# A selective-scan block on one core: step size and sums of states added by DMAs, x plus shift made in DRAM, a new timetable

## The chip, the core and the metric

The kernel runs on one core of one Trainium2 chip. The metric is the device time of one execution in microseconds (us); several executions are timed and their median is taken. The profile is of one further execution.

## What is computed

For four sequences of 4096 tokens with D = 512 channels, all in fp32:

```
h    = layernorm(x) * (1 + ca) + sa
xs,z = split(h @ w_in.T + b_in)
dt   = softplus(xs @ w_dt.T + b_dt);  Bm = xs @ w_B.T + b_B;  Cm = xs @ w_C.T + b_C
state[t] = exp(A*dt[t]) * state[t-1] + dt[t]*Bm[t]*xs[t]     (16 states per channel)
y    = sum over the 16 states of state[t]*Cm[t]  +  D*xs
x1   = x + ga * (layernorm((y*silu(z)) @ w_out.T + b_out + h) * gamma + beta)
out  = x1 + gb * (small feed-forward of layernorm(x1)*(1+cb)+sb)
```

## The kernel before, in words

The tokens are cut into 32 chunks of 512 (`NCH`), four blocks of 128 tokens each (`TB`), and the channels into four groups of 128 (`KD`). The scan of a chunk is U = 64 units, one for each of 16 states times four channel groups. For unit i:

- ACT makes the decay exp(A*dt) (`decays`, L915) five units ahead, and the input dt*xs*B in token-major form (`input_of`, L925);
- PE turns that input to channel-major form by four 128x128 transposes into PSUM (`turn_v`, L526 into `b_ps`). There are two buffers, so the transposes of unit i+1 wait for the scan of unit i-1;
- DVE scans (L1219), and keeps the last state of each pair (L1227);
- Pool multiplies two units at a time by C (`product`, L411) into the ring `pr` of 12 units.

The sum over the states goes two ways. For the states in `HELD`, the product of state n is not sent to PE: an accumulating DMA that Pool issues (`add_products`, L422, two units of 512 KB in all) adds it to the product of state n+1. What is left is added by PE as accumulating transposes into `y_ps` (`add_unit`, L601), four 128x128 instructions for each unit in `ADDS`: 40 units of a chunk. D*xs is added to state 3's product by DMAs too (`add_skip`, L429).

A step s scans chunk s, and beside it does the front of chunk f = s+1 (norm, `xs`, step size `dt`, B and C), the back of chunk b = s-1 (gate, `w_out`, second norm), and the feed-forward end of chunk c = s-2. All dense products run on PE in one fixed chain (`dense`). No scheduler orders this: every engine runs its 64 units in order, and a table of numbers says after which unit each other piece is put into the engine's program: `PE_AT` for PE's chain (`z.3.1@59` is the second product of z's fourth bank, after unit 59), `AT` for the rest. A piece stands in program order there, and everything behind it on its engine waits with it:

```
                for i in range(U):
                    if has_s and i + 1 < U:
                        turn_v(s, i + 1)
                    beside.until(i)
```

Three places the change touches:

- The step size. DVE makes max(v, 0) and -|v| (`take_dt`, L1290, L1296), ACT exp and ln of the second into `tmp` (`softplus`, L1057, L1060), Pool adds the halves (`step_size`, L474), then multiplies by xs (`inputs`, L485). PE turns the result (`turn_u`), DVE copies it (`take_u`, L1304), and ACT needs it for the first input of the next chunk.
- x plus shift. SP loads x again into `x1` (`loads`, L344), Pool issues two accumulating DMAs of the shift row (`shifted`, L446), waits for them and adds the attention part (`attended`, L454).
- The sums of states, above.

Of the kernel before, what the change touches and what calls it, by code (L numbers as in the profile page):

```python
def build_program(nc, ap, B, L, D, N, M, INNER):
# [46 lines left out]
    AT = dict(  # L48
        store=(0, 3, 5, 7),
        load=(2, 4, 8, 12),  # L50
        c_store=51,
        xsh=(13, 17),
        x1=(17, 17, 19, 19),
        bout=55,
        dt_add=(41, 42, 45, 49),
        u_mul=(43, 50, 50, 50),
        gate=(29, 60, 62, 6),
        relu=(61, 61, 0, 0, 0, 0, 0, 3),
        gm=4,
        skip=(6, 8, 9, 13),  # L60
        rstdx=11,
        xn=(11, 11, 11, 11),
        t2=(11, 13, 18, 21),
        rstd2=25,
        xn2=(25, 25, 25, 25),
        h2=(28, 32, 39, 42),
        h=(16, 20, 21, 22),
        xs=(25, 25, 26, 30),
        cb=50,
        bt=50,  # L70
        edt=(40, 43, 45, 50),
        ldt=(40, 43, 45, 50),
# [1340 lines left out]
```

## Time and profile before

| what | value |
|---|---|
| three timed executions | 4292.26, 4300.26, 4297.14 us; median 4297.14 |
| the profiled execution | 4280.81 us, its span 4279.1 us |
| granted TensorE clock, mean | 0.989 of full speed |
| busy share: PE, ACT, DVE, Pool | 96%, 89%, 85%, 83% |
| DMA traffic | 555.86 MB, mean 130 GB/s |

A busy share is a mean over the span, in which stretches with different limits lie. A row of a group of instructions gives line, engine, operation, tiles, count, busy time and the mean of one. A row of the timeline gives start and length; where the next row of the same engine starts sooner than the length says, instructions overlap, and the distance of the starts is what one costs.

### The profile page before, as it was taken

Reading aid. Unit: us, or ns where it says so; the run is one execution under the profiler, and the core shown is the slowest. Engines: PE = TensorE matmul, PEld = TensorE weight load, DVE = VectorE, ACT = ScalarE, POOL = GpSimd, SP = SyncE. Lnnn points to the kernel's source line nnn. Section 1 sums busy time; section 2 is a strip of 40 time slices with the busy share of each in tenths; the row PEclk is TensorE's granted clock in tenths of the full one; section 3 lists DMA queues with packets and bytes.
Section 4 is the critical chain, followed back from the end, with each engine's and each line's share of the span. In section 5 each row is a group of like instructions: output and inputs, shape, how many; then the busy total and the mean of one; then the engine's idle time right before and its main releaser. Section 6 shows DMA issues by size and latency. Waiting matters only on the chain. (4 is left out here: it accounts for less than half of the span.)

```text
span 4279.1 us, 70886 instructions
## 1 busy us (share of the span) xinstructions
PE 4100.2 (96%) x22688; PEld 2620.3 (61%) x22688; DVE 3643.8 (85%) x5134; ACT 3826.7 (89%) x6371; POOL 3558.1 (83%) x2090
## 2 busy tenths in 40 slices
PE   7999999999999999999999999999999999999987
PEld 3666666666666666666666666656666666666654
DVE  3788898888888888888888888888988888988884
ACT  3899999999999999998999999999999999999984
POOL 2888889888888888888888888988888888888883
PEclk8999999999999999999999999999999999999998
DMA  4456555656655666555666555665556675556663
GB/s 148 103 125 150 133 122 110 145 131 145 135 123 111 142 141 141 133 115 117 139 148 141 128 115 126 134 148 132 128 115 137 133 150 132 125 113 141 129 140 70
DMA packets 242537, 555.86 MB, mean 130 GB/s; under 512 B 29020, under 2 KB 31068, under 8 KB 242168
## 3 DMA queue, kind: packets, MB, share of 16 engines
q0 software_dynamic: 98816, 302.02, 39.1%
q1 hardware_dynamic: 143352, 249.29, 18.9%
q8 instruction: 185, 3.03, 0.3%
q14 instruction: 184, 1.51, 0.1%
HBM read 281.70 MB, written 34.64 MB: 74 GB/s over the span
## 5 line engine op out<-in xcount | busy, mean ns | idle before, releaser
L411 POOL TENSOR_TENSOR work<-work,c_bc 128x1024 f32<-128x1024 f32 x1024 | 2653.2, 2672 | 414.2 <-DVE work L1219 307.0
L1219 DVE TENSOR_TENSOR_SCAN work<-work,state,b_ps 128x512 f32<-128x512 f32 x1792 | 2245.6, 1272 | 242.2 <-PE b_ps L526 207.1
L925 ACT ACTIVATE work<-u_td,b_td 128x512 f32<-128x512 f32 x2048 | 1455.5, 711 | 114.7 <-PE b_ps L526 104.7
L915 ACT ACTIVATE work<-dt_t,neg_a 128x512 f32<-128x512 f32 x2048 | 1453.9, 710 | 17.1 <-DVE work L1219 14.7
L526 PEld LDWEIGHTS b_ps<-ident,work 128*128 128x128 f32 x8192 | 969.1, 141 | 645.1 <-issue 415.5
L526 PE MATMUL b_ps<-ident,work 128*128 128x128 f32 x8192 | 1229.1, 275 | 107.6 <-DVE work L1219 100.3
L601 PEld LDWEIGHTS y_ps<-ident,work 128*128 128x128 f32 x5120 | 585.9, 141 | 164.1 <-issue 157.1
L601 PE MATMUL y_ps<-ident,work 128*128 128x128 f32 x5120 | 673.4, 275 | 4.6 <-DMA work<-work 2.8
L675 PE MATMUL dense<-w_out_t,proj 128*128 128x512 f32 x1024 | 519.7, 606 | 0.0
L733 PE MATMUL dense<-xs_t,w_dt_t 128*128 128x512 f32 x1024 | 506.1, 593 | 0.0
L767 PE MATMUL dense<-h_t,w_in_t 128*128 128x512 f32 x1024 | 502.7, 593 | 0.0
L704 PE MATMUL dense<-h_t,w_in_t 128*128 128x512 f32 x1024 | 483.3, 595 | 1.0 <-ACT h_t L929 1.0
L422 POOL DMA_DIRECT2D work<-work x384 | 425.4, 1151 | 55.5 <-POOL work L411 46.5
L1219 DVE TENSOR_TENSOR_SCAN work<-work,b_ps 128x512 f32<-128x512 f32 x256 | 305.5, 1211 | 51.3 <-PE b_ps L526 49.8
L526 PEld LDWEIGHTS dense<-ident,xn 128*128 128x128 f32 x1536 | 187.7, 144 | 138.1 <-issue 88.1
L526 PE MATMUL dense<-ident,xn 128*128 128x128 f32 x1536 | 237.3, 279 | 34.1 <-ACT xn L1012 16.0
L474 POOL TENSOR_TENSOR dt_t<-dt_t,tmp 128x512 f32<-128x512 f32 x128 | 196.8, 1620 | 78.6 <-ACT tmp L1060 78.2
L704 PEld LDWEIGHTS dense<-h_t,w_in_t 128*128 128x128 f32 x1024 | 175.9, 191 | 127.7 <-issue 120.3
L947 ACT ACTIVATE tmp<-gm,b,w 128x512 f32<-128x512 f32 x256 | 196.4, 805 | 63.8 <-POOL sz_t L490 49.1
L675 PEld LDWEIGHTS dense<-w_out_t,proj 128*128 128x128 f32 x1024 | 162.1, 190 | 143.3 <-issue 143.3
L767 PEld LDWEIGHTS dense<-h_t,w_in_t 128*128 128x128 f32 x1024 | 167.1, 191 | 77.2 <-issue 67.7
L454 POOL TENSOR_TENSOR x<-x,tmp 128x512 f32<-128x512 f32 x128 | 206.9, 2006 | 2.3 <-DMA x<-par_d 2.3
(113 smaller groups left out, 4214.4 us busy)
## 6 DMA issues: line engine op xcount, KB each, us to landing
work<-work POOLq DMA_DIRECT2D x384, 512.0 KB, 5.7
c_bc<-c_d SPq DMA_DIRECT2D x512, 256.0 KB, 3.5
xn<-in_x SPq DMA_DIRECT2D x128, 256.0 KB, 5.1
work<-xs_t POOLq DMA_DIRECT2D x64, 512.0 KB, 5.9
x<-in_x SPq DMA_DIRECT2D x128, 256.0 KB, 4.4
x<-par_d POOLq DMA_DIRECT2D x64, 512.0 KB, 6.7
x<-par_d POOLq DMA_DIRECT2D x32, 1024.0 KB, 9.9
out_dram<-x SPq DMA_DIRECT2D x128, 256.0 KB, 4.2
```

Of the source, the lines that this page charges most:

```text
L411: gp.tensor_tensor(made_here, both(hs, HS_RING, s * U + i), c_bc[:, (s * N + n) % C_RING:(s * N + n) % C_RING + 1, :].to_broadcast([P, 2, ...
L422: gp.dma_start(both(pr, PR_RING, s * U + i), both(pr, PR_RING, s * U + i - KD), accum_op=ALU.add).then_inc(sum_done[i % KD // 2], Q)
L454: gp.tensor_tensor(x1[:, tb, :], x1[:, tb, :], tmp[:, tb, :], ALU.add).then_inc(S["x1_done"], 1)
L526: return nc.tensor.transpose(dst, src, ident[:, :])
L601: last = mm(y_ps[:, tb, j * P:(j + 1) * P], pr[:, (s * U + i) % PR_RING, tb * P:(tb + 1) * P], ident[:, :], is_transpose=True, start=(i == ...
L675: last = mm(long(s, "pre", tb)[:, :], yz_t[:, k, tb * P:(tb + 1) * P], w_out[:, k, :], start=False, stop=(k == KD - 1))
L704: last = mm(long(s, "xs", m)[:, :], w_in[:, k, m * P:(m + 1) * P], h_t[:, f % 2, k, :], start=(k == 0), stop=(k == KD - 1))
L733: last = mm(long(s, "dt", m)[:, :], w_dt[:, k, m * P:(m + 1) * P], xs_t[:, k, :], start=(k == 0), stop=(k == KD - 1))
L767: last = mm(long(s, "z", m)[:, :], w_in[:, k, D + m * P:D + (m + 1) * P], h_t[:, s % 2, k, :], start=(k == 0), stop=(k == KD - 1))
L915: A(decay[:, (s * U + i) % DEC_RING, :], dt_t[:, s % 2, j, :], ACT.Exp, scale=neg_a[:, j, n:n + 1]).then_inc(S["dec_done"], 1)
L925: A(v[:, n % V_RING, tb, :], u_td[:, tb, :], ACT.Copy, scale=b_td[:, s % 2, tb, n:n + 1]).then_inc(S["v_done"], 1)
L1219: V.tensor_tensor_scan(hs[:, (s * U + i) % HS_RING, :], decay[:, (s * U + i) % DEC_RING, :], b_ps[:, i % 2, :], state[:, i:i + 1] if s % N ...
```

## The change

1. `HELD` has eight states in place of six: 0, 1, 3, 4, 6, 7, 9, 10. So 16 accumulating DMAs of a chunk sum products in place of 12, and PE adds 32 units in place of 40.
2. The two halves of the step size are added by two accumulating DMAs of 512 KB each, issued by Pool, in place of four Pool instructions. Whoever waited for `dt_done` waits for `dt_added`.
3. x plus shift is made ahead in a DRAM buffer: at unit 40 of step s SP writes the shift row 512 times to DRAM (1 MB), at unit 59 Pool issues an accumulating DMA of x on it (1 MB, DRAM to DRAM), and in step s+1 SP loads the sum into `x1`. The two accumulating DMAs of `shifted` go.
4. All numbers of `PE_AT` and `AT` are new.

The diff, with most of the two tables left out:

```diff
--- before.py
+++ after.py
@@ -21,7 +21,7 @@
 
     V_RING, DEC_RING, HS_RING, PR_RING, C_RING = 2, 7, 6, 12, 3
 
-    HELD = (0, 1, 3, 4, 6, 8)
+    HELD = (0, 1, 3, 4, 6, 7, 9, 10)
     RELU_RING = 3
 
 
@@ -33,60 +33,61 @@
     GROUPS = ("g", "pre.0", "pre.1", "pre.2", "pre.3", "z.0", "xs.0", "xs.1", "xs.2", "xs.3", "dt.0", "dt.1", "dt.2",
               "dt.3", "cb", "z.1", "z.2", "s", "z.3")
     PE_AT = {}
-    for entry in """g.0@0 g.1@0 g.2@0 g.3@0 g.4@1 g.5@2 g.6@2 yz.0@2 g.7@3 res.0@3 yz.1@3 pre.0.0@4 yz.2@4 pre.0.1@5
...
-        z.1.1@49 bt.0@50 z.1.2@50 z.1.3@52 z.2.0@53 ut.0@55 z.2.1@55 z.2.2@55 ut.1@55 z.2.3@55 s.0@57 ut.2@57
-        s.1@57 s.2@57 ut.3@58 s.3@59 z.3.0@59 z.3.1@59 z.3.2@59 z.3.3@61""".split():
+    for entry in """g.0@0 g.1@1 g.2@3 g.3@3 g.4@8 g.5@8 g.6@8 yz.0@8 g.7@8 res.0@8 yz.1@8 pre.0.0@9 yz.2@9 pre.0.1@10
...
+        z.1.1@54 bt.0@55 z.1.2@56 z.1.3@57 z.2.0@58 ut.0@61 z.2.1@61 z.2.2@61 ut.1@61 z.2.3@61 s.0@62 ut.2@62
+        s.1@62 s.2@62 ut.3@62 s.3@62 z.3.0@63 z.3.1@63 z.3.2@63 z.3.3@63""".split():
         part, first = entry.split("@")
         PE_AT[part] = int(first)
     AT = dict(
-        store=(0, 3, 5, 7),
-        load=(2, 4, 8, 12),
-        c_store=51,
-        xsh=(13, 17),
-        x1=(17, 17, 19, 19),
...
-        dt_add=(41, 42, 45, 49),
-        u_mul=(43, 50, 50, 50),
...
-        xs=(25, 25, 26, 30),
...
-        y_copy=(1, 1, 1, 1),
-        yz=(2, 4, 5, 7),
...
-        dt=(35, 40, 43, 45),
-        ut=(54, 56, 57, 58),
...
-        stx=(0, 0, 6, 9),
...
+        store=(5, 10, 12, 17),
+        load=(11, 11, 15, 27),
+        c_store=45,
+        x1=(17, 19, 23, 28),
...
+        dt_add=(50, 53),
+        u_mul=(54, 56, 56, 56),
...
+        xs=(32, 35, 36, 39),
...
+        y_copy=(7, 7, 7, 7),
+        yz=(8, 9, 10, 11),
...
+        dt=(43, 47, 50, 53),
+        ut=(61, 61, 62, 62),
...
+        stx=(1, 8, 11, 11),
...
+        spread=40,
+        x_add=59,
     )
 
     def summed(n):
@@ -117,6 +118,7 @@
 
         par_d = nc.dram_tensor("par_d", (4, B, D), f32).ap()
         c_d = nc.dram_tensor("c_d", (2, N, T), f32).ap()
+        xsh_d = nc.dram_tensor("xsh_d", (2, TB, P, D), f32).ap()
 
         w_in = sb("w_in_t", [P, KD, 2 * D])
         w_dt = sb("w_dt_t", [P, KD, D])
...
@@ -341,8 +343,19 @@
                 for tb in range(TB):
                     yield AT["load"][tb]
                     sp.wait_ge(S[f"stored_{tb}"], at(f"stored_{tb}", c, Q))
-                    sp.dma_start(x1[:, tb, :], ap["x"][b * T + tb * P:b * T + (tb + 1) * P, :]
+                    sp.wait_ge(S["x_added"], (b + 1) * Q)
+                    sp.dma_start(x1[:, tb, :], xsh_d[b % 2, tb]
                                  ).then_inc(xb_loaded[tb], Q)
+
+            def spread_shift(s):
+                yield AT["spread"]
+                sp.wait_ge(S["par_stored"], 4 * Q)
+                if s >= 2:
+                    for tb in range(TB):
+                        sp.wait_ge(xb_loaded[tb], (s - 1) * Q)
+                sp.dma_start(xsh_d[s % 2].rearrange("b p d -> p b d"),
+                             par_d[1:2, s // NC:s // NC + 1, :].to_broadcast([P, TB, D])
+                             ).then_inc(S["shift_spread"], Q)
 
             def store_c(f):
                 yield AT["c_store"]
...
@@ -437,19 +452,17 @@
                     if summed(i // KD):
                         add_products(s, i)
 
-            def shifted(b):
-                for n in range(TB // 2):
-                    yield AT["xsh"][n]
-                    gp.wait_ge(S["par_stored"], 4 * Q)
-                    for tb in (2 * n, 2 * n + 1):
-                        gp.wait_ge(xb_loaded[tb], (b + 1) * Q)
-                    gp.dma_start(x1[:, 2 * n:2 * n + 2, :], par_d[1:2, b // NC:b // NC + 1, :].to_broadcast([P, 2, D]),
-                                 accum_op=ALU.add).then_inc(xsh_done[n], Q)
+            def add_x(s):
+                yield AT["x_add"]
+                gp.wait_ge(S["shift_spread"], (s + 1) * Q)
+                gp.dma_start(xsh_d[s % 2].rearrange("b p d -> p b d"),
+                             ap["x"][s * T:(s + 1) * T, :].rearrange("(b p) d -> p b d", p=P),
+                             accum_op=ALU.add).then_inc(S["x_added"], Q)
 
             def attended(b):
                 for tb in range(TB):
                     yield AT["x1"][tb]
-                    gp.wait_ge(xsh_done[tb // 2], (b + 1) * Q)
+                    gp.wait_ge(xb_loaded[tb], (b + 1) * Q)
                     gp.wait_ge(S["t2_done"], at("t2_done", b, tb + 1))
                     gp.tensor_tensor(x1[:, tb, :], x1[:, tb, :], tmp[:, tb, :], ALU.add
                                      ).then_inc(S["x1_done"], 1)
@@ -468,11 +481,11 @@
                 gp.tensor_tensor(wout_g[:, :], wout_g[:, :], wout_b[:, :], ALU.mult).then_inc(S["wout_done"], 1)
 
             def step_size(f):
-                for m in range(KD):
-                    yield AT["dt_add"][m]
-                    gp.wait_ge(S["ldt_done"], at("ldt_done", f, m + 1))
-                    gp.tensor_tensor(dt_t[:, f % 2, m, :], dt_t[:, f % 2, m, :], tmp[:, m, :], ALU.add
-                                     ).then_inc(S["dt_done"], 1)
+                for n in range(KD // 2):
+                    yield AT["dt_add"][n]
+                    gp.wait_ge(S["ldt_done"], at("ldt_done", f, 2 * n + 2))
+                    gp.dma_start(dt_t[:, f % 2, 2 * n:2 * n + 2, :], tmp[:, 2 * n:2 * n + 2, :], accum_op=ALU.add
+                                 ).then_inc(dt_added[n], Q)
 
             def inputs(f, b):
                 for m in range(KD):
...
@@ -910,7 +923,8 @@
                 n, j = i // KD, i % KD
                 if i == 0:
                     act.wait_ge(S["neg_done"], 2)
-                    act.wait_ge(S["dt_done"], at("dt_done", s, KD))
+                    act.wait_ge(dt_added[0], (s + 1) * Q)
+                    act.wait_ge(dt_added[1], (s + 1) * Q)
                 act.wait_ge(S["scan_done"], at("scan_done", s, i + 1 - DEC_RING))
                 A(decay[:, (s * U + i) % DEC_RING, :], dt_t[:, s % 2, j, :], ACT.Exp, scale=neg_a[:, j, n:n + 1]
                   ).then_inc(S["dec_done"], 1)
...
@@ -1314,7 +1328,7 @@
                     V.tensor_scalar(sz_t[:, m, :], bank[:, :], b_z[:, m:m + 1], None, ALU.add
                                     ).then_inc(S["zc_done"], 1)
                     if m:
-                        dve.wait_ge(S["dt_done"], at("dt_done", f, m + 1))
+                        dve.wait_ge(dt_added[m // 2], min(f + 1, NCH) * Q)
                     dve.wait_ge(S["x1_done"], at("x1_done", b, m + 1))
                     V.tensor_scalar(tmp[:, m, :], bank[:, :], b_z[:, m:m + 1], -87.0, ALU.add, ALU.max
                                     ).then_inc(S["zmax_done"], 1)
```

On PE, the end of one chunk and the first eight units of the next (`dense<-proj,win` is s, `dense<-h_t,w_in_t` z, `dense<-ident,xn` here the turn of u, `y_ps` the sum of states, `b_ps` the input of a unit, `dense<-tmp,w_dg` g). Before:

```order
L526 MATMUL dense<-ident,xn 128x128 x4
L526 MATMUL b_ps<-ident,work 128x128 x4
L791 MATMUL dense<-proj,win 128x512
L767 MATMUL dense<-h_t,w_in_t 128x512 x3
L526 MATMUL b_ps<-ident,work 128x128 x8
L767 MATMUL dense<-h_t,w_in_t 128x512
L601 MATMUL y_ps<-ident,work 128x128 x12
L526 MATMUL b_ps<-ident,work 128x128 x4
L601 MATMUL y_ps<-ident,work 128x128 x20
L526 MATMUL b_ps<-ident,work 128x128 x8
L623 MATMUL dense<-tmp,w_dg 64x256 x8
L601 MATMUL y_ps<-ident,work 128x128 x12
```

Eight units' sums (32 instructions) stand between z and g. In the change, the same place:

```order
L539 MATMUL b_ps<-ident,work 128x128 x4
L804 MATMUL dense<-proj,win 128x512
L539 MATMUL dense<-ident,xn 128x128 x4
L804 MATMUL dense<-proj,win 128x512 x2
L539 MATMUL dense<-ident,xn 128x128 x4
L804 MATMUL dense<-proj,win 128x512
L614 MATMUL y_ps<-ident,work 128x128 x4
L780 MATMUL dense<-h_t,w_in_t 128x512 x4
L614 MATMUL y_ps<-ident,work 128x128 x12
L539 MATMUL b_ps<-ident,work 128x128 x8
L636 MATMUL dense<-tmp,w_dg 64x256 x2
L539 MATMUL b_ps<-ident,work 128x128 x4
```

The products of s and z's last bank, and the turns of u, stand after units 61 to 63 now, with little between them but these; before, they were spread from unit 55 on. Behind them, in the change's first units of the next chunk:

```order
L636 MATMUL dense<-tmp,w_dg 64x256 x2
L539 MATMUL b_ps<-ident,work 128x128 x8
L636 MATMUL dense<-tmp,w_dg 64x256 x4
L539 MATMUL b_ps<-ident,work 128x128 x8
L614 MATMUL y_ps<-ident,work 128x128 x8
L539 MATMUL b_ps<-ident,work 128x128 x4
L614 MATMUL y_ps<-ident,work 128x128 x4
L539 MATMUL b_ps<-ident,work 128x128 x8
L636 MATMUL dense<-tmp,w_dg 64x256 x6
```

Half of g's products stand behind unit 8 now, and the turns of y behind them; before, all of g's products and the turns of y stood within the first eight units.

On Pool, the step size in the last third of a chunk. Before (`dt_t<-dt_t,tmp` is the add, `xn<-dt_t,xs_t` the product u, `work<-work,c_bc` the product of two units):

```order
L474 TENSOR_TENSOR dt_t<-dt_t,tmp 128x512 x2
L411 TENSOR_TENSOR work<-work,c_bc 128x1024
L485 TENSOR_TENSOR xn<-dt_t,xs_t 128x512
L411 TENSOR_TENSOR work<-work,c_bc 128x1024
L474 TENSOR_TENSOR dt_t<-dt_t,tmp 128x512
L411 TENSOR_TENSOR work<-work,c_bc 128x1024 x2
L474 TENSOR_TENSOR dt_t<-dt_t,tmp 128x512
L485 TENSOR_TENSOR xn<-dt_t,xs_t 128x512 x3
```

The products u follow their adds on the same engine, the last three directly. In the change, where the adds are DMAs:

```order
L487 DMA dt_t<-tmp 128x1024
L426 TENSOR_TENSOR work<-work,c_bc 128x1024 x2
L487 DMA dt_t<-tmp 128x1024
L498 TENSOR_TENSOR xn<-dt_t,xs_t 128x512
L426 TENSOR_TENSOR work<-work,c_bc 128x1024
L498 TENSOR_TENSOR xn<-dt_t,xs_t 128x512 x3
L426 TENSOR_TENSOR work<-work,c_bc 128x1024 x2
L474 DMA x<-par_d 128x4x512
L458 DMA xsh_d<-in_x 128x4x512
```

Three products u stand behind the second DMA, with one product of states between; the DMAs of the bias row and of x to DRAM follow together.

## Rows read from the trace of the kernel before

**Rows 1.** The page, engines: busy us, share of span, instructions.

```profile
PE 4100.2 (96%) x22688; PEld 2620.3 (61%) x22688; DVE 3643.8 (85%) x5134; ACT 3826.7 (89%) x6371; POOL 3558.1 (83%) x2090
```

**Rows 2.** One chunk in three stretches: stretch, length, busy by engine, clock, DMA share.

```profile
1629.41:1646.62 17.21, 14.81 (x105) 9.70 (x105) 17.02 (x25) 16.77 (x29) 11.31 (x7) 1.00 0.09 28
1646.62:1683.84 37.22, 37.22 (x163) 20.83 (x162) 33.38 (x52) 34.19 (x62) 29.10 (x22) 1.00 0.98 211
1683.84:1758.12 74.28, 74.16 (x444) 50.53 (x444) 63.28 (x85) 68.36 (x113) 70.91 (x42) 1.00 0.52 117
```

**Rows 3.** An instruction done once a chunk: first and last start.

```profile
L1046 ACT ACTIVATE cb_t<-dense,b_cb_col x32: 345/348/368, 57.9 to 4053.1; 128x128 f32<-128x128 f32 x32
```

**Rows 4.** Timeline of PE: start, length, what.

```profile
1499.88 2.22 PE L623 MATMUL dense<-tmp,w_dg 128*64 128x256 f32 x16
1502.03 1.53 PE L601 MATMUL y_ps<-ident,work 128*128 128x128 f32 x12
...
1604.13 0.60 PE L526 MATMUL b_ps<-ident,work 128*128 128x128 f32 x4
1604.57 1.02 PE L767 MATMUL dense<-h_t,w_in_t 128*128 128x512 f32 x2
1605.43 1.04 PE L601 MATMUL y_ps<-ident,work 128*128 128x128 f32 x8
```

**Rows 5.** Timeline of DVE, the same columns.

```profile
1637.88 2.44 DVE L1219 TENSOR_TENSOR_SCAN work<-work,state,b_ps 128x512 f32<-128x512 f32 x2
1640.24 0.13 DVE L1227 TENSOR_REDUCE state<-work 128x2 f32<-128x2 f32 x1
1640.29 0.68 DVE L1258 TENSOR_TENSOR proj<-sz_t,dense 128x512 f32<-128x512 f32 x1
1640.88 1.27 DVE L1219 TENSOR_TENSOR_SCAN work<-work,state,b_ps 128x512 f32<-128x512 f32 x1
```

**Rows 6.** Waits over the whole span: total us, times, longest.

```profile
POOL x L446 <- DMA x<-in_x: 116.5, 58, 12.4
...
DVE norm L1237 <- POOL x L454: 41.0, 33, 3.5
```

**Rows 7.** The page, DMA queues (share of 16 engines' span) and issues (us to landing).

```profile
q0 software_dynamic: 98816, 302.02, 39.1%
...
work<-work POOLq DMA_DIRECT2D x384, 512.0 KB, 5.7
...
x<-par_d POOLq DMA_DIRECT2D x32, 1024.0 KB, 9.9
```

**Rows 8.** Groups by line on Pool and ACT: busy us, mean ns, idle before.

```profile
L422 POOL DMA_DIRECT2D work<-work x384 | 425.4, 1151 | 55.5 <-POOL work L411 46.5 <-DMA work<-work 4.8 <-PE y_ps L601 3.3
L474 POOL TENSOR_TENSOR dt_t<-dt_t,tmp 128x512 f32<-128x512 f32 x128 | 196.8, 1620 | 78.6 <-ACT tmp L1060 78.2
...
L1057 ACT ACTIVATE tmp<-tmp,b_dt_col 128x512 f32<-128x512 f32 x128 | 91.3, 713 | 8.3 <-DVE tmp L1296 8.3
...
L1060 ACT ACTIVATE tmp<-tmp 128x512 f32<-128x512 f32 x128 | 80.9, 632 | 4.1
```

**Rows 9.** Timeline of Pool at the start and in the tail.

```profile
60.30 1.26 POOL L474 TENSOR_TENSOR dt_t<-dt_t,tmp 128x512 f32<-128x512 f32 x1 [2.45 <-ACT tmp L1060]
...
4246.71 2.48 POOL L454 TENSOR_TENSOR x<-x,tmp 128x512 f32<-128x512 f32 x2 [2.33 <-DMA x<-par_d]
```

**Rows 10.** Stretches of the second chunk's start, columns as in rows 2.

```profile
213.40:219.50 6.10, 2.85 (x21) 2.17 (x21) 6.03 (x12) 2.60 (x5) 2.36 (x1) 0.98 0.31 86
219.50:222.80 3.30, 3.30 (x17) 3.30 (x18) 3.30 (x5) 3.27 (x6) 1.54 (x1) 0.53 0.00 0
222.80:240.00 17.20, 15.33 (x75) 9.03 (x74) 16.58 (x27) 15.55 (x28) 14.55 (x10) 1.00 0.64 149
```

**Rows 11.** Timeline of PE in that low stretch.

```profile
219.49 1.09 PE L526 MATMUL b_ps<-ident,work 128*128 128x128 f32 x4 [0.62 <-DVE work L1219]
...
221.22 1.06 PE L526 MATMUL dense<-ident,dt_t 128*128 128x128 f32 x4
```

More of the change, by code:

```diff
@@ L67, in build_program @@
-        h=(16, 20, 21, 22),
-        xs=(25, 25, 26, 30),
[L69 to L72, printed above, removed]
-        ez=(24, 57, 57, 4),
-        lz=(24, 57, 57, 4),
-        sig=(24, 57, 57, 5),
-        y_copy=(1, 1, 1, 1),
-        yz=(2, 4, 5, 7),
-        out=(9, 10, 11, 13),
-        pre=(9, 11, 14, 18),
-        dt=(35, 40, 43, 45),
-        ut=(54, 56, 57, 58),
-        z=(21, 53, 56, 61),
-        s=59,
-        stx=(0, 0, 6, 9),
-        nmrx=10,
@@ L86, in build_program @@
-        st2=(23, 23, 23, 24),
-        nmr2=25,
-        y=(14, 14, 18, 24, 28, 28, 34, 34, 36, 37, 40, 40, 45, 46, 46, 46, 46, 46, 46, 47, 47, 51, 52, 52, 54, 54, 55, 56, 57, 61, 61, 61, 62, 62, 62, 62, 62, 64, 64, 64),
-        sum=(6, 8, 9, 11, 13, 17, 17, 20, 21, 25, 30, 32, 39, 40),
+        store=(5, 10, 12, 17),
+        load=(11, 11, 15, 27),
+        c_store=45,
+        x1=(17, 19, 23, 28),
+        bout=59,
+        dt_add=(50, 53),
+        u_mul=(54, 56, 56, 56),
+        gate=(42, 62, 63, 8),
@@ new lines, in build_program @@
+        relu=(62, 63, 1, 1, 3, 7, 7, 7),
+        gm=7,
+        skip=(0, 3, 8, 12),
+        rstdx=14,
+        xn=(14, 14, 15, 16),
+        t2=(17, 18, 23, 24),
+        rstd2=33,
+        xn2=(33, 33, 33, 33),
+        h2=(38, 40, 44, 49),
+        h=(23, 25, 26, 29),
+        xs=(32, 35, 36, 39),
+        cb=54,
+        bt=54,
+        edt=(49, 50, 50, 52),
+        ldt=(49, 50, 50, 52),
+        ez=(39, 58, 60, 8),
+        lz=(39, 58, 60, 8),
+        sig=(39, 58, 60, 8),
+        y_copy=(7, 7, 7, 7),
@@ new lines, in build_program @@
+        yz=(8, 9, 10, 11),
+        out=(12, 14, 16, 20),
+        pre=(12, 17, 21, 23),
+        dt=(43, 47, 50, 53),
+        ut=(61, 61, 62, 62),
+        z=(27, 58, 61, 63),
+        s=62,
+        stx=(1, 8, 11, 11),
+        nmrx=13,
+        st2=(21, 31, 31, 31),
+        nmr2=32,
+        y=(16, 16, 20, 21, 30, 31, 31, 33, 41, 42, 43, 44, 52, 52, 52, 53, 53, 54, 55, 58, 59, 59, 59, 60, 61, 62, 63, 63, 63, 69, 69, 70),
+        sum=(5, 7, 10, 12, 13, 18, 18, 21, 23, 26, 29, 31, 34, 37, 42, 43, 45, 47),
@@ L200, in build_program @@
         w2dg_done b_out_loaded bout_done moved_ps moved c_exp c_one c_rcp silu_c rows_ps rows_taken mods_ps mods_done sign_done gate_done par_made
-        par_stored bout_row bout_made bout_added gs_loaded wg_loaded wout_done sign_set""".split()
+        par_stored shift_spread x_added bout_row bout_made bout_added gs_loaded wg_loaded wout_done sign_set""".split()
         PER = {
             "SP": dict(stored_0=Q, stored_1=Q, stored_2=Q, stored_3=Q, c_stored=TB * Q),
-            "Pool": dict(prod_done=U // 2, x1_done=TB, dt_done=KD, u_done=KD, sz_done=KD),
+            "Pool": dict(prod_done=U // 2, x1_done=TB, u_done=KD, sz_done=KD),
             "PE": dict(b_made=U, y_added=len(ADDS), s_ps=1, g_used=J, yz_ps=KD, out_ps=TB, res_used=TB, pre_ps=TB, xt_ps=KD, xs_ps=KD,
@@ L361, in step @@
                     chains.append(loads(b, c))
+                if has_s:
+                    chains.append(spread_shift(s))
                 if has_f:
```

37 lines of the change are left out of this document (13 added, 24 removed).

## The prediction

> **What bounds the kernel now.** I read the engines' shares first: PE is busy 96% of the span, ACT 89%, DVE 85%, Pool 83% [rows 1]. That makes PE the suspect but says nothing of where. So the next view is the table of stretches, cut for one chunk at the starts of the scans of units 0, 8 and 24 and of the next chunk's unit 0 [rows 2]. It shows three limits. In units 0 to 7 (17.2 us) DVE is busy 17.0 and PE 14.8. In units 8 to 23 (37.2) PE is busy throughout and the DMA engines are at 0.98. In units 24 to 63 (74.3) PE is busy 74.2 and the DMA share is 0.52. A chunk takes 128.7 us there; over the run it is (4053.1 - 57.9) / 31 = 128.9 [rows 3].
>
> PE's and DVE's work can be counted out of the two tables of numbers. What one piece costs is the distance of starts in the timelines. On PE: four 128x128 turns or sums of a unit 0.43 to 0.44, a 128x512 product (two records) 0.86, one of g's eight parts 2.15 / 4 = 0.54 [rows 4]; an `out` product I put at 1.05, since it stands between changes of tile. On DVE: a scan with its share of the state copy (1640.29 - 1637.88) / 2 = 1.2, a multiply or copy of 128x512 0.59 [rows 5]; estimates beside these are 0.87 for a pair of moments, 0.67 for the scaling behind, 1.3 for the two reads of a bank of dt or z; the counts below bear them out. Before:
> - units 0 to 7: PE 16 groups of four, 2 products, 8 of g = 13.0; DVE 8 scans, 8 copies, 3 moments = 17.1. Measured 17.2.
> - units 8 to 23: PE 26 groups, 23 products, 4 `out` = 35.4; DVE 32.9. Measured 37.2, so 1.8 is lost.
> - units 24 to 63: PE 82 groups, 43 products, B and C = 74.4; DVE 61.6. Measured 74.3.
> So the larger of PE and DVE in each stretch, plus 1.8, gives the chunk. PE and DVE can't borrow from each other over more than two units, since the transposes of unit i+1 wait for the scan of unit i-1.
>
> **The change part by part.**
> *Two more states summed.* PE loses 8 units of 4 instructions: 8 x 0.437 = 3.5 us a chunk, the only work that leaves PE. Pool issues four more DMAs, at most 1.15 us each [rows 8]; traffic grows by 2 MB a chunk.
> *Step size by DMA.* Four Pool adds of 1.62 [rows 8] become two issues. Over the whole change Pool gets five issues more (four sums, two step sizes, x, less the two of the shift), 5.8 us, and loses 6.5: no difference on an engine with 111 of 128.7 busy [rows 2]. What counts is latency. A DMA of that size from Pool lands 5.7 us after its issue [rows 7], where an add took 1.26 [rows 9]. Behind the second one stand three products u, which PE's turn of u and so everything of units 61 to 63 waits for. PE has 21 groups, 5 products, and B and C between the last product of dt (unit 52) and that turn: 9.2 + 4.3 + 1.4 = 14.9 us. The chain beside it is DVE 1.3, exp and ln 0.71 + 0.63 [rows 8], issue 1.15 [rows 8], landing 5.7, and three products at the add's 1.26 = 13.3, plus up to 3.7 for a scan and a product of states that are in front. Slack is 1.6 to -2.1; I take it as hidden, with a stall of 0 to 2.
> *x plus shift ahead.* Two accumulating DMAs of 512 KB leave the crowded stretch; 1 MB to DRAM by SP at unit 40 and 1 MB of accumulation at unit 59 come where the share was 0.52 [rows 2]. No row shows a DRAM-to-DRAM accumulation. Bounds: nothing, and the 9.9 us of the 1 MB one into SBUF [rows 7] once more; it has some 25 us until the load that waits for it, so both ends are hidden and I take 0. Pool stops waiting for x (116.5 us in all) and DVE's moments for x1 (41.0, or 1.3 a chunk) [rows 6].
> *Traffic.* The software queue used 39.1% of 16 engines for 302 MB [rows 7], 5.5 us for each MB. Units 8 to 23 lose the shift's 1 MB, one sum and a load, so their share falls from 0.98 to near 0.8; units 24 to 63 gain four sums, two step sizes and x, 4 MB or 22 us, beside SP's 1 MB, and go from 0.52 to near 0.8.
> *The timetable.* The dense chain starts some seven units later and ends at unit 63. Counted as above, after:
> - units 0 to 7: PE 11 groups and 4 of g = 7.0; DVE 8 scans, 4 copies, 1 moment = 12.9.
> - units 8 to 23: PE 29 groups, 17 products, 4 of g, 4 `out` = 33.7; DVE 33.9.
> - units 24 to 63: PE 76 groups, 51 products, B and C = 78.6; DVE 64.6.
> So the 3.5 us that leave PE mostly don't leave the stretch where PE is the limit: that one grows by 4.2, since eight products have moved into it. What is gained is 4.2 of DVE's time in units 0 to 7, where PE will stand idle half the time, and some of the middle.
> *Sum.* 12.9 + 33.9 + 78.6 = 125.4 with no loss. The middle lost 1.8 before, with DMAs full; now the DMAs are freer but PE and DVE have the same amount, so each wait of one on the other counts: I take 2.2. For the end, with ACT's second norm and the step size, 0.5. That is 128.1, against 128.9: 0.8 less, 25 us over 31 chunks.
> *Start and tail.* The first chunk's step size is on the path: Pool's last add at 60.3 is followed at once by the products u [rows 9]. A landing of 5.7 and its issue stand in place of 1.3, and u's first product comes behind it: +6. In the tail the last additions to x waited 2.33 for the shift [rows 9]: -2.
> Together -21 us: 4281 becomes 4260 in a profiled execution. That one lay 16 us below the median of the three, so on the medians 4297 - 21 = **4276 us**.
>
> A rule on DMAs beside this: the Trainium skill ("DMA: Bandwidth & Descriptors", "Anatomy of one DMA — SWDGE (gpsimd) path") fits 2.0 us plus bytes / 436e3 to such a DMA, an estimate of 3.2 us for 512 KB. The rows show 5.7 for the accumulating ones; by the page the chain of the step size would be 2.5 us shorter and never late, and the sum the same.
>
> **The rivals.**
> 1. *PE's saving comes out whole.* Nothing is lost in any stretch: 125.4 a chunk, 3.5 less; -108 + 4 us, 4193. For it: units 24 to 63 lost nothing before, and the middle's 1.8 may have been the full DMA engines. Against: PE and DVE have never had equal work over 16 units here.
> 2. *The step size comes late (slower).* The second DMA lands over some 7.5 us after its issue; then PE stands before the turn of u, and all of s, z's last banks and the next chunk's first unit behind it wait too. Bounds: the slack above at its low end, 2.1 late, and a landing of 9.9 as for 1 MB [rows 7] at the same time, 6 late. I price 3: 131.1, +2.2 a chunk; +68 + 4 us, 4369. For it: the chain has five hops between four engines and units 24 to 63 have more DMAs. Against: the last sum is issued after unit 47.
> 3. *PE and DVE trip over each other in the middle (slower).* Turns of y, `out` and the first norms alternate between them. Loss 4.4 in place of 2.2: 130.3, +1.4; +43 + 4 us, 4344.
> 4. *The clock falls in the thin units.* In the second chunk the granted clock was 0.53, the lower of its levels (1.2 GHz), for 3.3 us, after 6.1 us with PE busy 2.85 [rows 10]; the record of four turns was 1.06 to 1.09 then, where it is 0.60 at 2.4 GHz [rows 4, 11]. Units 0 to 7 will have PE at 7.0 of 13 us. One such dip a chunk costs between nothing (DVE is the limit there) and 1.65 us: 4276 to 4327; I put 4305. The Trainium skill ("TensorE: Matmul & The Clock Gate", "Part 4: PE-mode transpose") says that transposes don't count as PE-busy for the clock. By that rule the dip would come in every chunk, as five in seven of PE's pieces there are turns or sums. The trace speaks against it: the clock was back at 222.8 after nothing but transposes, which is why the chance is small.
> That the change does not do what it says is no rival: the order of the instructions has 32 sums a chunk and the two DMAs.
>
> **How the numbers follow.** A measurement of this kernel can tell about 0.2% (8.6 us) from no change. Forecast 0.40 (its own range 4245 to 4300: 0.33 faster, 0.05 same, 0.02 slower); rival 1 0.15; rival 2 0.20; rival 3 0.17 (0.03 same); rival 4 0.08 (0.04 same). Faster 0.48, same 0.12, slower 0.40. The range runs from rival 1 to just under rival 2, 4190 to 4365: half of each of them is left out, less than 2 in 10.
>
> **What would show it.** Right: in a chunk cut as above, units 0 to 7 near 13 us with DVE full and PE near 7, the middle near 36, the rest near 79 with PE full, and no wait of PE for u over 2 us. Rival 1: middle 34. Rival 2: PE idle before the turn of u, released by Pool's product u, and Pool waiting on the DMA of the step size. Rival 3: middle over 38 with waits of PE on DVE's scaling. Rival 4: clock under 1.00 in the first stretch of most chunks. The forecast is wrong at its root if units 24 to 63 take under 77 us: then PE's work can't be counted this way.

## The result and the profile after

The change makes the kernel slower: 4334.99 us (median of 4 runs, 4331.32 to 4338.83) against 4295.69 beside it (4292.26 to 4300.26), a ratio of 1.0091, 95% interval 1.0073 to 1.0108. The forecast was 4276.

The page after, first the engines' shares [rows 1], then the software queue and four kinds of DMA with their KB and us to landing [rows 7]:

```profile
PE 4049.7 (93%) x21664; PEld 2511.5 (58%) x21664; DVE 3635.9 (84%) x5134; ACT 3826.1 (88%) x6371; POOL 3538.7 (82%) x2122
...
q0 software_dynamic: 125952, 402.70, 50.5%
...
work<-work POOLq DMA_DIRECT2D x512, 512.0 KB, 5.0
...
dt_t<-tmp POOLq DMA_DIRECT2D x64, 512.0 KB, 5.3
...
xsh_d<-par_d SPq DMA_DIRECT2D x32, 1024.0 KB, 10.5
xsh_d<-in_x POOLq DMA_DIRECT2D x32, 1024.0 KB, 18.0
```

PE is busy 50 us less in a span 54 us longer. So the time is in waits of PE, and the span is cut as before [rows 3], by ACT's instruction done once a chunk:

```profile
L1060 ACT ACTIVATE cb_t<-dense,b_cb_col x32: 343/347/367, 59.5 to 4111.3; 128x128 f32<-128x128 f32 x32
```

(4111.3 - 59.5) / 31 = 130.7 us a chunk against 128.9: +57. What lies ahead of the first is 1.6 longer; what lies behind the last is 4333.0 - 4111.3 = 221.7 against 226.0, 4.3 shorter. That is the whole difference of the spans, 4333.0 - 4279.1 = 54; the medians differ by 39 only, since the profiled execution of the kernel before lay 15 us below the 4295.69.

Next the same chunk in the three stretches of [rows 2], with units 52 to 55 by themselves as a fourth row (columns: stretch, length, busy us of PE, PEld, DVE, ACT and Pool, granted clock, DMA share, GB/s):

```profile
1661.80:1674.82 13.02, 10.22 (x75) 6.20 (x73) 12.92 (x17) 13.02 (x21) 9.01 (x5) 1.00 0.70 176
1674.82:1710.37 35.55, 33.91 (x166) 19.64 (x162) 34.05 (x54) 32.72 (x59) 30.18 (x20) 1.00 0.82 189
1710.37:1794.12 83.75, 81.29 (x439) 51.84 (x439) 66.40 (x91) 73.73 (x121) 71.20 (x43) 0.98 0.73 146
1758.60:1771.55 12.95, 10.74 (x82) 7.02 (x82) 6.42 (x9) 7.58 (x13) 11.05 (x8) 0.87 0.70 129
```

Over the third to the 31st chunk the means of the stretches are 12.98, 35.57 and 81.99; before they were 17.04, 37.67 and 74.43, and the forecast 12.9, 36.1 and 79.1. Two of three terms came true. The loss is in units 24 to 63. In this chunk PE is idle there for 2.5 us, nearly all of it in units 52 to 55 (12.95 long, PE busy 10.74), and its clock is low there.

The waits over the whole span name what came last (total us, times, longest):

```profile
POOL work L437 <- DMA work<-work: 129.8, 34, 6.1
...
PE y_ps L614 <- DMA work<-work: 58.4, 36, 3.1
```

Before, Pool waited for sums 4.8 us in all at the issue of the next [rows 8]. The timelines of Pool, SP and PE in this chunk show the place (start, length, what; in brackets the idle time before, and its releaser):

```profile
1742.88 0.87 POOL L437 DMA_DIRECT2D work<-work  x1 [0.30 <-POOL work L426]
...
1747.69 0.87 POOL L437 DMA_DIRECT2D work<-work  x1 [0.30 <-POOL work L426]
1748.41 2.54 POOL L426 TENSOR_TENSOR work<-work,c_bc 128x1024 f32<-128x1024 f32 x1
1754.77 0.86 POOL L437 DMA_DIRECT2D work<-work  x1 [3.82 <-DMA work<-work]
1755.38 2.65 POOL L426 TENSOR_TENSOR work<-work,c_bc 128x1024 f32<-128x1024 f32 x1
1758.33 0.88 POOL L437 DMA_DIRECT2D work<-work  x1 [0.30 <-POOL work L426]
```

```profile
1740.39 1.10 SPq L356 DMA_DIRECT2D xsh_d<-par_d  x1
```

```profile
1760.77 1.10 PE L614 MATMUL y_ps<-ident,work 128*128 128x128 f32 x8
1764.07 0.66 PE L614 MATMUL y_ps<-ident,work 128*128 128x128 f32 x4 [2.21 <-DMA work<-work]
```

SP issues the 1 MB write of the shift at 1740.39; it lands 11.1 us later. Beside it run the two sums into the state of units 40 to 43, issued at 1742.88 and 1747.69. They land 11.4 and 9.5 us after their issue, where a sum takes 5.0 in the median; over the 29 chunks these two have the same medians, 11.4 and 9.5, and the longest took 13.6. The third sum adds that state to the next, so it can't be issued before the first has landed: Pool stands until 1754.77. The fourth follows at 1758.33, and PE, which adds this next state to y at unit 52, stands until 1764.07.

The DMA share of the whole stretch, 0.73, hides the crowd. From the issue of the first of these sums to its landing the share is 0.97:

```profile
1742.88:1754.24 11.36, 11.22 (x62) 7.33 (x61) 10.22 (x14) 11.23 (x19) 7.77 (x5) 1.00 0.97 174
```

A cut around PE's wait shows the rest:

```profile
1760.19:1764.56 4.37, 2.16 (x29) 1.73 (x29) 2.23 (x3) 3.83 (x8) 4.37 (x4) 1.00 0.90 170
1764.56:1768.12 3.56, 3.56 (x25) 1.69 (x23) 1.33 (x2) 2.19 (x4) 3.56 (x4) 0.54 0.34 63
1768.12:1771.55 3.43, 3.43 (x26) 2.90 (x25) 1.28 (x1) 0.00 (x0) 1.53 (x2) 0.98 0.93 165
```

After that wait the granted clock is 0.54, near the lower level of 1.2 GHz, for 3.56 us in which PE is busy throughout. Such a dip followed in 8 of the 29 chunks, and units 52 to 55 took 13.0 us in those and 10.3 in the others.

**Theory A**: the write of the shift at unit 40 lies on the chain of sums, and the loss is there. **Rivals**: the eight products more in units 24 to 63, which the forecast counted too cheap; the landing of the step size's DMAs; and y's adds packed into units 59 to 63.

### The profile page after: what moved, and what is told of

It is laid out like the page before. It is cut to its first block and busy times, and to the rows that moved or that the text cites. A ratio compares the mean times of both kernels' runs of the same rounds, so it can differ in the third digit from the quotient of the medians.

```text
span 4333.0 us, 69121 instructions
## 1 busy us (share of the span) xinstructions
PE 4049.7 (93%) x21664; PEld 2511.5 (58%) x21664; DVE 3635.9 (84%) x5134; ACT 3826.1 (88%) x6371; POOL 3538.7 (82%) x2122
## 5 line engine op out<-in xcount | busy, mean ns | idle before, releaser
L437 POOL DMA_DIRECT2D work<-work x512 | 478.1, 934 | 227.2 <-DMA work<-work 129.8
L614 PEld LDWEIGHTS y_ps<-ident,work 128*128 128x128 f32 x4096 | 485.9, 142 | 260.8 <-issue 185.2
L614 PE MATMUL y_ps<-ident,work 128*128 128x128 f32 x4096 | 578.6, 276 | 58.4 <-DMA work<-work 58.4
L780 PE MATMUL dense<-h_t,w_in_t 128*128 128x512 f32 x1024 | 514.4, 605 | 1.2 <-issue 0.9
L688 PE MATMUL dense<-w_out_t,proj 128*128 128x512 f32 x1024 | 509.7, 600 | 0.0
L717 PE MATMUL dense<-h_t,w_in_t 128*128 128x512 f32 x1024 | 488.1, 595 | 1.0 <-ACT h_t L943 1.0
L503 POOL TENSOR_TENSOR sz_t<-sz_t,tmp 128x512 f32<-128x512 f32 x128 | 218.6, 1708 | 89.5 <-ACT tmp L1085 89.5
L467 POOL TENSOR_TENSOR x<-x,tmp 128x512 f32<-128x512 f32 x128 | 193.1, 1508 | 18.9 <-DMA x<-xsh_d 10.5
## 6 DMA issues: line engine op xcount, KB each, us to landing
xn<-in_x SPq DMA_DIRECT2D x128, 256.0 KB, 10.7
```

Source lines behind the costliest of these rows:

```text
L437: gp.dma_start(both(pr, PR_RING, s * U + i), both(pr, PR_RING, s * U + i - KD), accum_op=ALU.add).then_inc(sum_done[i % KD // 2], Q)
L503: gp.tensor_tensor(sz_t[:, m, :], sz_t[:, m, :], tmp[:, m, :], ALU.mult).then_inc(S["sz_done"], 1)
L614: last = mm(y_ps[:, tb, j * P:(j + 1) * P], pr[:, (s * U + i) % PR_RING, tb * P:(tb + 1) * P], ident[:, :], is_transpose=True, start=(i == ...
L688: last = mm(long(s, "pre", tb)[:, :], yz_t[:, k, tb * P:(tb + 1) * P], w_out[:, k, :], start=False, stop=(k == KD - 1))
L717: last = mm(long(s, "xs", m)[:, :], w_in[:, k, m * P:(m + 1) * P], h_t[:, f % 2, k, :], start=(k == 0), stop=(k == KD - 1))
L780: last = mm(long(s, "z", m)[:, :], w_in[:, k, D + m * P:D + (m + 1) * P], h_t[:, s % 2, k, :], start=(k == 0), stop=(k == KD - 1))
```

## Experiments

The kernel before, timed beside each group of runs, had medians of 4289.6 to 4295.7 us; each ratio is to it. So a difference between runs of two groups is uncertain by up to 6 us, and is given below as a range, from the ratios and from the times. Stretch means are over the same 29 chunks.

**1. The write ten units later.** After the last sum.

```
-        spread=40,
+        spread=50,
```

> The change with SP's 1 MB write of the shift row to DRAM issued at unit 50 in place of unit 40, behind the sums of states. Theory A (that write shares the DMA engines with the sums of state 10, which then land after 11.6 us where 5.0 is usual; Pool waits for them before it can issue the next sums, and PE waits at unit 52 for those): Pool's waits for sums fall from 130 us to under 30, PE's waits for sums from 58 us to under 10, units 24 to 63 go from 82.0 to about 79.5, time 4335 - 2.2 x 31, about 4265. Rival B (the chain of sums 40, 44 is too tight in itself, whatever else moves): waits stay over 80 us, time within 10 us of 4335.

Measured: 4258.42 us, ratio 0.9927 [0.9911, 0.9944], 31 us below the kernel before and 70 to 77 below the changed kernel. One chunk of it, the last two rows of the cut, and Pool's sums of the same units:

```profile
1677.15:1756.88 79.73, 79.47 (x439) 51.22 (x439) 66.39 (x90) 73.63 (x121) 71.32 (x43) 1.00 0.71 153
1725.39:1734.33 8.94, 8.94 (x82) 6.42 (x82) 6.43 (x10) 7.47 (x13) 8.16 (x6) 1.00 0.58 110
```

```profile
1709.66 0.87 POOL L437 DMA_DIRECT2D work<-work  x1 [0.30 <-POOL work L426]
...
1714.48 0.87 POOL L437 DMA_DIRECT2D work<-work  x1 [0.30 <-POOL work L426]
1715.20 2.55 POOL L426 TENSOR_TENSOR work<-work,c_bc 128x1024 f32<-128x1024 f32 x1
1718.06 0.86 POOL L437 DMA_DIRECT2D work<-work  x1 [0.30 <-POOL work L426]
```

The third sum is issued 8.4 us after the first and waits for no DMA; units 52 to 55 take 8.9 us and PE is busy for all of it. The first sum lands after 4.6 us, and in as long a time from its issue the DMA share is 0.74:

```profile
1709.66:1721.02 11.36, 11.21 (x62) 7.30 (x61) 10.21 (x14) 11.24 (x19) 10.77 (x7) 1.00 0.74 144
```

The means are 12.98, 35.56, 79.69: only the last stretch has changed, by 2.3 us a chunk. Theory A holds. The 50 in the table is not where the write starts: in SP's program it stands behind transfers that wait for ACT and Pool, and all chunks but the first and the last have it at unit 57, where the step size's DMAs have landed.

```profile
1736.16 0.54 SPq L356 DMA_DIRECT2D xsh_d<-par_d  x1
```

So this run says nothing of the write beside the step size's DMAs.

**2. The write far ahead.** At unit 2 of the chunk, and still at 40 in the first.

```
-        spread=40,
+        spread=2,
...
-                yield AT["spread"]
+                yield AT["spread"] if s else 40
```

> The change with SP's 1 MB write issued at unit 2 in place of unit 40 (in the first scanned chunk at 40, since the row is not in DRAM before). Theory A (only the meeting with the sums costs, and at unit 2 the DMA engines are nearly idle): like unit 50, 4258 within 12 us, units 24 to 63 near 79.7 and Pool's waits for sums under 30 us. Rival F (at unit 2 it meets the first sums at units 5 to 10 as it met those at 42): the middle or the first stretch grows by 1 us or more, 4285 or more.

Measured: 4263.69, ratio 0.9941 [0.9926, 0.9955]; 12.98, 35.57, 79.70. A place before the sums serves as well as one after them. SP runs ahead of the scan here and issues the write during the last unit of the chunk before; it takes 14.3 us in the median, and no engine waits for it. The first scanned chunk, which keeps its collision, takes 147.1 us here and 140.8 in run 1: 6 us for it. The second chunk starts at 225.8 here, 217.6 in run 1, 223.2 in the changed kernel and 211.6 before.

**3. A second write that nothing needs.** Run 1 with another 1 MB written by SP at unit 40.

```
+        dummy=40,
...
+            def dummy_write(s):
+                yield AT["dummy"]
...
+                sp.dma_start(dum_d.rearrange("b p d -> p b d"),
+                             par_d[1:2, s // NC:s // NC + 1, :].to_broadcast([P, TB, D])
+                             ).then_inc(S["dummied"], Q)
```

> The changed kernel with the write of the shift at unit 50 (4258.4 us), plus a second write that nothing needs: SP writes another 1 MB of the broadcast shift to a DRAM buffer of its own at unit 40, where the changed kernel had its write. Nothing waits for it but SP, one chunk later. Theory A (the 1 MB write beside the sums issued at units 42 to 47 is the loss, whatever it is for): Pool waits 3 to 4 us for a sum before it issues the next, PE before y's adds at unit 52, units 52 to 55 go from 8.9 to 11 us, and the time returns to 4325 to 4345. Rival B (what counted was that the shift was in DRAM early, or the order of SP's other DMAs): within 10 us of 4258.

Measured: 4340.43, ratio 1.0101 [1.0086, 1.0116]; 12.98, 35.56, 82.25, units 52 to 55 11.3. The two waits are back (the lines have moved by 13):

```profile
POOL work L450 <- DMA work<-work: 133.1, 34, 6.4
...
PE y_ps L627 <- DMA work<-work: 65.2, 38, 3.9
```

So it is the write as traffic, not what it writes nor SP's order around it: 75 to 82 us for a transfer that does nothing. In runs 1 to 3 theory A is shown from both sides.

**4. What PE's work in units 24 to 63 is worth.** Run 1 with the old six held states, so eight groups of y's adds and four sums fewer: the only part of the change taken back.

```
-    HELD = (0, 1, 3, 4, 6, 7, 9, 10)
+    HELD = (0, 1, 3, 4, 6, 8)
...
-        sum=(5, 7, 10, 12, 13, 18, 18, 21, 23, 26, 29, 31, 34, 37, 42, 43, 45, 47),
+        sum=(5, 7, 10, 12, 13, 18, 18, 21, 23, 26, 29, 31, 38, 40),
```

> The changed kernel with the write of the shift at unit 50 (4258.4 us when it was run), and of the change the two more summed states taken back: HELD has six states, so PE adds 40 products to y instead of 32 (the eight more at units 37 to 40 and 45 to 49) and Pool issues 14 sums instead of 18. All else, the new timetable above all, stays. Theory A (PE's instructions are the time of units 24 to 63): 8 groups of four at 0.437 us = 3.5 us a chunk more, all of it in units 24 to 63: these go from 79.7 to 83.2, and the time to 4258 + 108 = 4366 us. Rival B (PE waits there for others and the adds fill its waits, as the eight adds that were moved out of units 59 to 63 gave only 0.6 of their 3.5 us): at most 1.5 us a chunk, 4258 to 4305. Fewer DMAs could give something back in either case.

Measured: 4373.31, ratio 1.0178 [1.0163, 1.0193], 108 to 115 above run 1; 12.98, 35.56, 83.60. One chunk:

```profile
1726.70:1810.34 83.64, 82.92 (x471) 54.90 (x471) 66.80 (x90) 73.83 (x121) 67.80 (x39) 1.00 0.59 120
```

PE is busy 82.92 where run 1 has 79.47: 3.45 us, the eight groups at 0.437 of the forecast, and the time follows, with 0.4 a chunk more in waits. The two more summed states are worth their full price in the new timetable.

**5. The step size added by Pool again**, in the changed kernel, as `dt_add=(49, 50, 51, 53)`.

> The change with the halves of the step size added by Pool again, at units 49, 50, 51, 53. Theory A (the two DMAs are hidden in all chunks but the first): the start is some 5 us shorter, the rest the same; 4335 within 12 us. Rival E (the DMA of the step size comes late for the turn of u): units 24 to 63 lose 2 us or more, 4275 or less.

Measured: 4367.83, ratio 1.0179 [1.0164, 1.0194], 33 to 38 above the changed kernel, which neither of my two cases had; units 60 to 63 take 17.6 us in place of 16.4. The wait of PE's turn of u:

```profile
PE dense L539 <- POOL xn L498: 36.5, 25, 5.6
```

In the changed kernel that wait is 7.4 us, once, at the start. So here the four adds on Pool, at the one set of places that was tried, make u late, and the DMAs don't: the opposite of my second rival.

**6. The step size by DMA alone**, in the kernel before. The second issue at unit 49 and the products u moved behind it (the expectation names their old units):

```
-        dt_add=(41, 42, 45, 49),
-        u_mul=(43, 50, 50, 50),
+        dt_add=(43, 49),
+        u_mul=(48, 52, 53, 53),
```

> The kernel before with one part of the change alone: the step size is added by two accumulating DMAs instead of four Pool adds; timetable, six held states and the shift's DMAs stay. Pool's four adds of 1.62 us (6.5 us a chunk) become two issues of at most 1.15 us. Putting the adds back into the changed kernel had cost 33 us (4367.8 against 4335.0). Theory A (the step size by DMA helps where Pool is close to being waited for and nothing waits for its landing): in the old timetable 50 units pass before the turns of u at unit 54 to 58, with products u at 43 and 50, so u's first product at unit 43 now waits for the landing: nothing to -20 us, 4270 to 4290. Rival B (the landing is what counts, as in my second rival): the turn of u comes late by 1 to 3 us a chunk, 4320 to 4380, with PE waiting before the turns and units 52 to 55 or 56 to 59 above the 5.9 and 8.0 us of the kernel before.

Measured: 4475.90, ratio 1.0419 [1.0403, 1.0434]; 17.04, 37.59, 80.61. The slower case, Rival B, and beyond its size. (The 5.9 and 8.0 us in the expectation are units 48 to 51 and 52 to 55; units 56 to 59 took 9.7 before.) In one chunk, Pool and then PE:

```profile
1808.11 0.87 POOL L474 DMA_DIRECT2D dt_t<-tmp  x1 [1.13 <-PE y_ps L601]
...
1812.29 2.65 POOL L411 TENSOR_TENSOR work<-work,c_bc 128x1024 f32<-128x1024 f32 x1
1814.60 2.77 POOL L485 TENSOR_TENSOR xn<-dt_t,xs_t 128x512 f32<-128x512 f32 x2
```

```profile
1817.42 1.12 PE L526 MATMUL dense<-ident,xn 128*128 128x128 f32 x4 [3.94 <-POOL xn L485]
```

The last two products u come 6.5 us after the issue and PE's turn of u, at unit 55 in this timetable, stands 3.9 us for them, and 132.0 in the whole span, in every chunk. The clock falls behind it (1.12 us for four turns, against 0.60). That is one half of my second rival's sign. The other, Pool waiting for the DMA, is missing. The landing of this DMA, and Pool's waits for such landings in the whole span:

```profile
DMA to landing us min/median/max: 4.6/4.6/4.6
```

```profile
POOL xn L485 <- DMA dt_t<-tmp: 7.4, 3, 3.9
```

The DMA has landed 1.9 us before the last two products start, here and in the mean of the 29 chunks. What stands in front of them is a product of states and their own place, unit 53 in place of 50. So the run shows what a late u costs, but the price is not that of the landing alone: with the products right behind it they would end near 1815.4 us, and PE would stand about 2 us less (an estimate from these rows).

**7, 8. Eight held states in the old timetable**, with y's adds moved as far as the sums ask; the second try has the last sums one to two units earlier and the adds later.

```
-        sum=(6, 8, 9, 11, 13, 17, 17, 20, 21, 25, 30, 32, 39, 40),
+        sum=(6, 8, 9, 11, 13, 17, 17, 20, 21, 25, 30, 32, 35, 38, 42, 44, 47, 49),
```

> The kernel before, its timetable kept, with eight held states alone (and the places of sums and of PE's additions that follow from it). Theory A (time is PE's count in units 24 to 63 plus DVE's in units 0 to 7): PE loses 3.5 us in units 24 to 63, which go from 74.3 to about 71, the other stretches stay; time 4296 - 108, about 4190. Rival C (what PE saves comes back as waits for DMAs or on other engines): under 30 us of it is seen, 4265 or more.

> As the second experiment (the old timetable, eight held states alone), but state 11's sums issued a unit or two earlier and PE's additions of it two units later, since PE waited 176 us for them there. Theory A (PE's count in units 24 to 63): those go from 74.4 to 71 to 72.5, time 4290 - 60 to -108, 4185 to 4230. Rival C (a chain of three sums in a row, each waiting for the one before, can't be hidden in the old timetable's short units 44 to 52): PE still waits over 60 us for sums, time over 4290.

Measured: 4515.29, ratio 1.0517 [1.0499, 1.0535], and 4526.90, ratio 1.0551 [1.0535, 1.0567]. In the first PE waits for sums before y's adds

```profile
PE y_ps L601 <- DMA work<-work: 175.6, 62, 5.8
```

and units 52 to 55 take 15.6 us. In the second those waits are gone, and PE waits for Pool's products u in their place, 90.5 us in 32 waits; units 52 to 59 take 23.7 us, where they took 17.7. In both runs theory A, built on PE's 3.5 us alone, missed by far; the second's rival C had the slower time, but not for its reason. In a chunk of the first Pool is busy for 74.2 of 82 us in the last stretch, where it had 70.9 before: a DMA that Pool issues also takes Pool's time, and the four adds of the step size are still with it. That this is why u comes late in the second run is argued, not shown.

**9. x plus shift ahead alone**, in the kernel before, with `spread=45, x_add=59`.

> The kernel before with x plus shift made ahead in DRAM alone (write at unit 45, behind the last sums at 40; x added at unit 59). Theory A: Pool's waits for x go (116 us, of which DVE's moments waited 41), and the DMA engines are relieved in units 8 to 23, which go from 37.7 to about 36.3: -1.3 x 31, about 4250. Rival H (the DRAM to DRAM traffic costs as much elsewhere): within 10 us of 4290.

Measured: 4281.68, ratio 0.9980 [0.9971, 0.9990]; 17.75, 36.10, 75.50. The middle stretch gives 1.6 us a chunk, and the two others take 1.8 of it back, so that the pace hardly changes (129.36 against 129.15): the part is worth about nothing by itself, as rival H said. In units 0 to 7 the DMA share was 0.09 and is 0.41, and DVE's moments, which this timetable has at unit 0, wait for SP's loads of x in one unit:

```profile
1636.63 0.69 DVE L1250 BATCH_NORM_STATS2 norm<-xn 128x6 f32<-128x512 f32 x1 [0.72 <-DMA xn<-in_x]
```

These loads run beside the 1 MB accumulation and take 8.1 us in the median, before 5.1; 23 of the chunks have such a wait, of up to 1.6 us. It is a second neighbour of the same kind, and the new timetable, which has three of the four moments at units 8 to 11, doesn't meet it.

**10, 11, 12. The end of the chunk.** Four of y's adds moved out of units 62 and 63 in the changed kernel; seven out of 59 to 63 in run 1 (the expectation says eight, but one of them only goes from unit 59 to 60); and the first turn of u with its neighbours one unit earlier in run 1.

```
-...59, 59, 59, 60, 61, 62, 63, 63, 63, 69, 69, 70),
+...59, 59, 59, 60, 61, 65, 65, 66, 66, 69, 69, 70),
```

> The change with four of PE's additions (16 instructions) moved from units 62 and 63 to units 1 and 2 of the next chunk. Theory A (a PE instruction costs its time in units 24 to 63 and nothing in units 0 to 7, where DVE is the limit): 4 x 0.437 = 1.75 us a chunk less, 54 us, about 4281; units 0 to 7 stay at 13.0. Rival D (PE's work is the limit everywhere, so that it makes no difference where it stands): units 0 to 7 grow by what the end loses, time within 10 us of 4335.

Measured: 4323.13, ratio 1.0073 [1.0058, 1.0088], 8 to 12 below the changed kernel; 13.06, 35.92, 81.08. The last stretch gives 0.9 us of the 1.75 and the middle takes 0.35 back, which is neither of my cases.

```
-...58, 59, 59, 59, 60, 61, 62, 63, 63, 63, 69, 69, 70),
+...58, 59, 60, 64, 64, 65, 66, 66, 67, 67, 69, 69, 70),
```

> The first experiment (write at unit 50) with eight of PE's additions moved from units 59 to 63 to units 0 to 3 of the next chunk. The four moved earlier gave 12 us, since DVE's reads of z's last bank stand between PE's last product and the next scan and had hidden three of them. Theory A: the four from units 59 to 62 beyond those now count, 4 x 0.437 = 1.7, with the 0.4 of before 2.1 a chunk, 65 us: 4190 to 4215. Rival G (units 60 to 63 are held by a chain PE, DVE, ACT of the turns of u, not by PE's work): under 20 us, 4240 or more.

Measured: 4264.63, ratio 0.9946 [0.9930, 0.9963]; 13.84, 35.55, 79.05: the end gives 0.6 and units 0 to 7 take 0.9. The time is what rival G said.

```
-ut.0@61 z.2.1@61 z.2.2@61 ut.1@61 z.2.3@61 s.0@62
+ut.0@60 z.2.1@60 z.2.2@60 ut.1@61 z.2.3@61 s.0@61
...
-        ut=(61, 61, 62, 62),
+        ut=(60, 61, 62, 62),
```

> The changed kernel with the write of the shift at unit 50 (4258.4 us), and in addition PE's first turn of u and the products z.2.1 and z.2.2 at unit 60 instead of 61, s.0 at 61 instead of 62, and DVE's first copy of u at 60 instead of 61. In that kernel Pool's last product u of chunk 12 was done at 1740.04 and PE's first turn came at 1742.28, so 2.2 us are free there. Theory A (the chain of turns, copies and the transposes of u in units 60 to 63 sets the end of the chunk): 0.5 to 1 us a chunk less, 4228 to 4243. Rival B (the work of DVE and PE between units 60 and 63 is what counts, in whatever order): within 8 us of 4258. Rival C (u is not there in time in most chunks): PE waits for it, 4270 or more.

Measured: 4256.77, ratio 0.9908 [0.9892, 0.9925]; 12.98, 35.56, 79.61. Rival B: the same as run 1. The last stretch of the two kernels, the adds moved first, the turns earlier second:

```profile
1679.89:1758.99 79.10, 77.91 (x417) 48.48 (x417) 66.31 (x90) 72.98 (x120) 70.77 (x43) 1.00 0.74 151
```

```profile
1676.01:1755.64 79.63, 79.42 (x439) 51.29 (x439) 66.43 (x91) 73.64 (x121) 71.34 (x43) 1.00 0.74 152
```

With the adds moved, PE's work in the stretch falls by 22 instructions and 1.6 us only (79.47 to 77.91), so not all seven had run in it, and 1.2 us is idle now where it was 0.3: another chain takes over at once. Which one of u's turns, DVE's copies and ACT it is, these runs don't settle. With the turns earlier PE is full, as before.

## Why the prediction was wrong

Forecast -21 us, measured +39; the sum's 128.1 us a chunk became 130.53.

- **Units 0 to 7: 12.9.** Measured 12.98, DVE busy 12.92. Right. PE had 10.2 there, not the counted 7.0: three parts of g that are written behind unit 8 run before its scan, and four turns that stand alone take 0.66 us, not 0.44. It cost nothing, since DVE is the limit there.
- **Units 8 to 23: 33.9 and a loss of 2.2, 36.1.** Measured 35.57: DVE 34.05, PE 33.91, loss 1.5. Right within 0.5.
- **Units 24 to 63: 78.6 and a loss of 0.5, 79.1.** Measured 81.99. This is the term that failed, and 2.3 of the 2.9 is one sentence of the step "x plus shift ahead": that the 1 MB to DRAM by SP at unit 40 comes "where the share was 0.52", so "both ends are hidden and I take 0". I bounded the transfer by whether its own reader would wait. It has none that does. What waited was a neighbour: the sums that run beside it. The step "Traffic" put the stretch near 0.8 of the DMA engines and so saw no crowding. The mean is 0.73 here, but beside the write it is 0.97, and the chain of a sum, its successor and y's add has slack for a landing of 5.0 us and not for 11.4. So a term that I put at nothing cost 70 to 77 us in all. With the write elsewhere the stretch is 79.69 and the sum 128.23, 0.1 from the forecast; that this is so close is luck, since the middle was 0.5 better than forecast and this stretch still 0.6 worse: PE is busy for 79.5 in the chunk of run 1, where I had counted 78.6 and 0.5 of loss.
- **Two more states summed: 3.5 us of PE a chunk.** Right: 3.45 in PE's busy time, 108 to 115 us in all (run 4).
- **Step size by DMA: a stall of 0 to 2.** No stall after the first chunk. It also gave what I had put at no difference: without it u is late and 33 to 38 us are lost (run 5). I had compared Pool's total, not its last 14 units, in which the adds stand in front of u.
- **Start: +6 to the first chunk, tail: -2.** The first scan comes 2.4 later, not 6, since the products of the first half of the step size now run during the second's landing. But the first chunk has the collision too, and the second starts 11.6 later (6.0 in run 1). The tail by the once-a-chunk instruction is 4.3 shorter.

The rivals. The first (all of PE's saving, middle 34) is false. The second is false here; in the old timetable PE did stand for u (run 6), but Pool did not stand for the DMA, as that rival had it. The third is false: the middle was better than forecast. The fourth is false in its place: units 0 to 7 of steady chunks have clock 1.00, though PE is busy for 10.2 of 13.0 us and mostly with turns and sums. But dips came in units 52 to 55, behind a wait. The slower side, 0.40 in all, had no case with this mechanism, though 4335 lies in the range.

The root test, units 24 to 63 not under 77 us, held: PE's work can be counted this way, and the count says what the timetable can give. Alone, in the old timetable, a part gives at most 8 us or costs 180 to 237 (runs 6 to 9); together, with one number changed, they give 31.

## What to carry to other kernels

A transfer that is moved has two prices: whether its reader waits, and whether it lengthens a chain of short transfers beside it that has little slack. List what is in flight during its whole landing, and put it where no transfer is that something waits for. The mean DMA share of a stretch doesn't show this; the share in the few microseconds of the landing does. And a step that adds latency to save an engine's time is worth what the schedule around it has room for: test it in the schedule that it is meant for, never in the old one alone.
